# Attention and experts on one core: the product with V a pair later, three probability buffers, and another check of the weights' low halves

## The reference

```python
codes = jnp.sign(v) * FP4_GRID[idx]          # FP4_GRID = 0, 0.5, 1, 1.5, 2, 3, 4, 6
scale = jnp.exp2(e)                          # a power of two for each block of 32 rows
w = codes * jnp.repeat(scales, block_size, axis=0)
q = _mxfp4_matmul(x, wq_codes, wq_scales) + bq       # k, v alike
attn = jax.nn.softmax(einsum('bqhd,bkhd->bhqk', q, k) / sqrt(128), axis=-1)
out = einsum('bhqk,bkhd->bqhd', attn, v)
...
x = x + _layernorm(attention(_layernorm(x)))
x = x + _layernorm(experts(_layernorm(x)))
```

## Time and profile before

| | |
|---|---|
| Executions shown | 1331.55, 1329.47, 1333.42 us |
| Median | 1331.55 us |
| Span of the profiled execution (first to last instruction) | 1341.9 us |
| Own time of the profiled execution, beside its span | not given apart from the three above |
| PE busy | 1207.5 us (90%) |
| POOL, DVE, ACT busy | 931.0, 860.6, 825.8 us (69, 64, 62%) |
| First scores, scores of pair 12, last scores (pair 127) | 30.7, 142.3, 977.0 us |
| End of the last WO | 993.6 us |

### The profile page before, as it was taken

How to read it: one execution, slowest core, us unless ns; L and a number is a source line. 1 busy time by engine, 2 the same in 40 slices (tenths; PEclk the granted TensorE clock), 3 DMA queues, 4 the chain that set the end, 5 groups by cost and what they waited for, 6 DMA issues and landing times.

```text
span 1341.9 us, 25318 instructions
## 1 busy us (share of the span) xinstructions
PE 1207.5 (90%) x7852; PEld 844.1 (63%) x7852; DVE 860.6 (64%) x2297; ACT 825.8 (62%) x2128; POOL 931.0 (69%) x1130
## 2 busy tenths in 40 slices
PE   4889999999999999989999999998958799989995
PEld 1556666666666666657666666665635378777973
DVE  5898567687678768767876876777676233222226
ACT  3666678768777776877777677777745133223413
POOL 4896456678878877986888798688764624444557
PEclk9899999999999999999999999999989899999998
DMA  7774987755555354354534545434445359898676
GB/s 257 173 191 94 228 211 150 163 102 120 122 99 118 73 116 94 73 108 82 93 68 98 97 69 94 79 70 81 81 100 165 112 166 259 226 234 213 131 211 227
DMA packets 364678, 182.68 MB, mean 136 GB/s; under 512 B 287440, under 2 KB 343222, under 8 KB 364544
## 3 DMA queue, kind: packets, MB, share of 16 engines
q1 hardware_dynamic: 344960, 166.18, 52.5%
q0 software_dynamic: 16416, 11.70, 4.9%
q10 hardware_dynamic: 3168, 3.15, 0.7%
HBM read 75.32 MB, written 64.69 MB: 104 GB/s over the span
## 4 chain that ended last, share of the span: by engine, by line
PE 39%; DVE 18%; DMA 14%; POOL 13%; issue 7%; ACT 5%; another core or an unknown queue 2%; SPq 1%; ACTq 0%; POOLq 0%; DVEq 0%
DMA PT<-PH 8%; PE bank L1066 7%; PE bank L1037 6%; PE bank L1081 6%; DMA Y<-W,wix 5%; POOL PH L972 4%; POOL P L967 4%; PE bank L1052 4%; PE bank L1098 3%; PE bank L1206 3%; DVE nm L1455 3%; PE bank L1219 2%; POOL BUF L716 2%; PE bank L1130 2%
## 5 line engine op out<-in xcount | busy, mean ns | idle before, releaser
L967 POOL TENSOR_SCALAR P<-P,rr 128x256 f32<-128x256 f32 x512 | 249.2, 498 | 141.2 <-DVE rr L1451 132.2
L1308 ACT ACTIVATE P<-bank,nm 128x256 f32<-128x256 f32 x512 | 237.2, 468 | 149.2 <-DVE nm L1455 140.9
L972 POOL TENSOR_TENSOR PH<-P,PH 128x512 f16<-128x512 f32 x256 | 296.2, 1171 | 20.1 <-ACT PH L1317 19.1
L1037 PE MATMUL bank<-RB,W 128*128 128x512 f16 x1076 | 257.9, 382 | 7.2 <-ACT Sx L645 4.2
L716 POOL DMA_INDIRECT BUF<-RT,ix x192 | 197.8, 1030 | 91.3 <-issue 42.2
L1066 PE MATMUL bank<-RB 128*128 128x256 f32 x1024 | 245.7, 383 | 2.7 <-issue 2.5
L1081 PE MATMUL bank<-PT,RB 128*128 128x256 f16 x1536 | 197.2, 273 | 36.1 <-DMA PT<-PH 32.1
L1455 DVE TENSOR_REDUCE nm<-bank 128x2 f32<-128x512 f32 x256 | 174.3, 682 | 51.1 <-PE bank L1066 50.5
L1081 PEld LDWEIGHTS bank<-PT,RB 128*128 128x128 f16 x1536 | 145.1, 98 | 95.9 <-DMA PT<-PH 50.5
L1066 PEld LDWEIGHTS bank<-RB 128*128 128x128 f32 x1024 | 185.7, 191 | 26.2 <-issue 3.8
L1317 ACT ACTIVATE PH<-P 128x512 f16<-128x512 f32 x256 | 161.4, 630 | 55.7 <-POOL P L967 38.9
(11 more groups left out here) (207 smaller groups left out, 1600.0 us busy)
## 6 DMA issues: line engine op xcount, KB each, us to landing
RB<-in_ewT SPq DMA_DIRECT2D x24, 352.0 KB
BUF<-zrow SPq DMA_DIRECT2D x4, 1926.0 KB, 8.4
W<-BUF SPq DMA_DIRECT2D x64, 120.4 KB
HT<-in_ewT SPq DMA_DIRECT2D x18, 352.0 KB
HT<-in_wc SPq DMA_DIRECT2D x24, 256.0 KB, 4.3
HT<-in_ws SPq DMA_DIRECT2D x24, 256.0 KB, 4.7
Y<-zrow SPq DMA_DIRECT2D x10, 512.0 KB, 3.5
RB<-in_ewd SPq DMA_DIRECT2D x24, 176.0 KB
```

What stands on the lines that cost most here:

```text
L967: r = eng.tensor_scalar(p, p, rr[:, w % 4, t:t + 1], SP_, ALU.mult, ALU.mult)
L972: eng.tensor_tensor(PH[:, w % 2, 1, :], P[:, w % 2, :], PH[:, w % 2, 0, :], ALU.subtract).then_inc(s["pl"], 1)
L1037: r = eng.matmul(bk_[:, :], W[:, m, a, c * 2048 + h * 128:c * 2048 + (h + 1) * 128], XT[:, bp % 2, b, c, :], start=(k == 0), stop=(k == n ...
L1308: r = eng.activation(P[:, u % 2, t * 256:(t + 1) * 256], bS[u % 2][:, t * 256:(t + 1) * 256], ACT.Exp, bias=nm0[:, u % 4, t:t + 1], accum_ ...
```

## The change

`ORDER` moves PV two slots on (units w-3 and w-4 rather than w-1 and w-2), WO two slots (w-5, w-6), the halves of O likewise (ACT 3 to 5, DVE 4 to 6), and puts V between Q and K. `PH` and `PT` get a third buffer (`NPT`), which lies in `SSf`; the load that stood there is moved to SP's slot 232 and to `XN`. So the turning DMA of unit w waits for PV of w-3, and the high half of w for the DMA of w-3. `P` keeps two buffers, and Pool's order of work on probabilities is the same. The background tables are laid out anew; the 24 scatters, for one, stand in slots 34 to 59 rather than 32 to 55. The loop is two slots longer. The check of a job's low half is one `tensor_reduce` with max over its 256 words, to one column for each job; the sign bit is not cleared any more.

```diff
@@ -19,7 +19,7 @@
 E = 64
 CAP = 96
 NST = 8
-W_AT = (0, 0, 1, 2, 2, 3, 4, 5, 5, 6, 7, 7, 8, 9, 10, 10, 11, 12, 12, 13, 14, 15, 15, 16)
+W_AT = (0, 0, 1, 2, 2, 3, 5, 6, 6, 7, 7, 9, 10, 10, 11, 13, 14, 15, 15, 16, 17, 17, 17, 17)
 W_LEAD = (1, 1, 2)
...
-NOSIGN = 0x7FFF7FFF
...
+NPT = 3
...
-ORDER = {
-    "pe": ([("S", 0), ("S", -1), ("Q", -2), ("K", -2), ("WO", 4), ("WO", 3), ("V", -6), ("PV", 2), ("PV", 1),
-                ("bg", 0)],
-           [("bg", 0)]),
-    "act": ([("exp", 0), ("bg", 0), ("exp", -1)],
-           [("Q", -1), ("P", 1), ("V", -5), ("P", 0), ("O", 3), ("bg", 0)]),
-    "dve": ([("max", 0), ("O", 4), ("max", -1), ("bg", 0), ("recip", 0), ("bg", 0), ("bg", 0)],
-           [("bg", 0), ("recip", 0), ("K", -1), ("bg", 0), ("V", -5), ("bg", 0)]),
-    "pool": ([("bg", 0)],
-           [("norm", 1), ("norm", 0), ("P", 1), ("P", 0), ("bg", 0)]),
-    "sp": ([("bg", 0), ("T", 1)],
-           [("bg", 0), ("T", 1)]),
-}
+ORDER = {'pe': ([('S', 0), ('S', -1), ('Q', -2), ('V', -6), ('K', -2), ('PV', 4), ('PV', 3), ('WO', 6), ('WO', 5),
+         ('bg', 0)],
+        [('bg', 0)]),
+ 'act': ([('exp', 0), ('exp', -1), ('bg', 0)],
+         [('bg', 0), ('Q', -1), ('P', 1), ('V', -5), ('P', 0), ('bg', 0), ('O', 5)]),
+ 'dve': ([('max', 0), ('O', 6), ('max', -1), ('recip', 0), ('bg', 0)],
+         [('recip', 0), ('bg', 0), ('K', -1), ('bg', 0), ('V', -5), ('bg', 0)]),
+ 'pool': ([('bg', 0)], [('norm', 1), ('norm', 0), ('P', 1), ('P', 0), ('bg', 0)]),
+ 'sp': ([('bg', 0), ('T', 1)], [('bg', 0), ('T', 1)])}
...
-PE_AT = (17, 19, 23, 31)
-STORE_AT = (18, 20)
+PE_AT = (19, 20, 25, 33)
+STORE_AT = (24, 34)
...
-KEEP_AT = (22, 24)
+KEEP_AT = (19, 26)
...
-        "pool": ((11, 0), (11, 0), (11, 2), (11, 4), (32, 0), (33, 4), (34, 0), (37, 0), (37, 0), (38, 0),
+       'pool': ((13, 0), (13, 0), (13, 2), (13, 3), (34, 0), (35, 0), (36, 0), (39, 0), (39, 0), (39, 4),
+                (40, 0), (42, 0), (42, 0), (43, 1), (46, 0), (48, 0), (48, 0), (50, 0), (51, 4), (53, 0),
+                (53, 0), (53, 3), (53, 4), (54, 0), (56, 0), (56, 0), (58, 0), (59, 0))}}
...
+        SSh = SSf[:, :].bitcast(F16)
+        PHB = [PH[:, 0, :, :], PH[:, 1, :, :], SSh[:, 0:1024].rearrange("p (l n) -> p l n", l=2)]
+        PTB = [PT[:, 0, :, :, :, :], PT[:, 1, :, :, :, :],
+               SSh[:, 1024:2048].rearrange("p (l t c q) -> p l t c q", l=2, t=2, c=2)]
...
-        lowbits = C1[:, :, :].rearrange("p t e -> p (t e)").bitcast(U32)
+        lowmax = C1[:, 0, 0:32]
...
-        sdf = SSf[:, 0:768].rearrange("p (j n) -> p j n", j=3)
+        sdf = XN[:, 0:3, :]
...
                 eng.wait_ge(s["wl"], n + 1)
-                if n == 0:
-                    eng.tensor_scalar(lowbits, lo.bitcast(U32), NOSIGN, None, ALU.bitwise_and).then_inc(s["lf"], 1)
-                else:
-                    eng.wait_ge(s["lf"], n)
-                    eng.scalar_tensor_tensor(out=lowbits, in0=lo.bitcast(U32), scalar=NOSIGN, in1=lowbits,
-                                             op0=ALU.bitwise_and, op1=ALU.bitwise_or).then_inc(s["lf"], 1)
...
-                return eng.tensor_reduce(low1, lowbits, AX, ALU.max)
+                return eng.tensor_reduce(low1, lowmax, AX, ALU.max)
...
                 eng.wait_ge(s["pl"], w + 1)
-                if w >= 2:
-                    eng.wait_ge(s["pv"], w - 1)
-                eng.dma_start_transpose(PT[:, w % 2, :, :, :, :].rearrange("p l t c q -> p (l t c) q"),
-                                        PH[:, w % 2, :, :].rearrange("p l n -> p (l n)")).then_inc(s_pt[w % 2], 16)
+                if w >= NPT:
+                    eng.wait_ge(s["pv"], w - NPT + 1)
+                eng.dma_start_transpose(PTB[w % NPT].rearrange("p l t c q -> p (l t c) q"),
+                                        PHB[w % NPT].rearrange("p l n -> p (l n)")).then_inc(s_pt[w % NPT], 16)
...
+                if slot == 232:
+                    eng.wait_ge(s["xc"], XC.n)
                     eng.dma_start(sdf[:, 0:2, :], sdT[0:256, :].rearrange("(j p) n -> p j n", p=128)
...
-                eng.tensor_tensor(PH[:, w % 2, 1, :], P[:, w % 2, :], PH[:, w % 2, 0, :], ALU.subtract
+                eng.tensor_tensor(PHB[w % NPT][:, 1, :], P[:, w % 2, :], PHB[w % NPT][:, 0, :], ALU.subtract
...
-                eng.wait_ge(s_pt[u % 2], 16 * (u // 2 + 1))
+                eng.wait_ge(s_pt[u % NPT], 16 * (u // NPT + 1))
...
-                                       PT[:, u % 2, b, :, kc, :], start=(k == 0), stop=(k == 5))
+                                       PTB[u % NPT][:, b, :, kc, :], start=(k == 0), stop=(k == 5))
...
             def p_high(w):
+                if w >= NPT:
+                    eng.wait_ge(s_pt[w % NPT], 16 * (w // NPT))
                 eng.wait_ge(s["pn"], w + 1)
-                if w >= 2:
-                    eng.wait_ge(s_pt[w % 2], 16 * (w // 2))
-                eng.activation(PH[:, w % 2, 0, :], P[:, w % 2, :], ACT.Copy).then_inc(s["ph"], 1)
+                eng.activation(PHB[w % NPT][:, 0, :], P[:, w % 2, :], ACT.Copy).then_inc(s["ph"], 1)
```

More of the change, by code:

```diff
@@ L108 @@
 X_SHIFT = 12
-PE_AT = (17, 19, 23, 31)
-STORE_AT = (18, 20)
+PE_AT = (19, 20, 25, 33)
+STORE_AT = (24, 34)
 PROLOGUE = {"act": "wxwwxwxww", "dve": "xxxxxxxxxxxxxxxxxwxwxwwww"}
-KEEP_AT = (22, 24)
[L115 to L123, removed]
[6 rows of a table removed]
-        "act": ((9, 5), (9, 5), (9, 5), (10, 0), (15, 4), (16, 0), (16, 2), (17, 2), (18, 0), (19, 4), (24,
-                0)),
-        "pool": ((11, 0), (11, 0), (11, 2), (11, 4), (32, 0), (33, 4), (34, 0), (37, 0), (37, 0), (38, 0),
-                (38, 0), (40, 0), (41, 1), (41, 2), (43, 1), (45, 0), (46, 0), (46, 0), (46, 0), (49, 0), (49,
-                1), (49, 4), (49, 4), (51, 4), (52, 0), (54, 0), (54, 0), (55, 3)),
-    },
-}
+KEEP_AT = (19, 26)
+PLACE = {'x': {'dve': ((1, 3), (1, 5), (2, 1), (2, 3), (2, 4), (3, 0), (3, 2), (3, 3), (3, 3), (4, 4), (4, 4), (4, 4),
+               (4, 4), (5, 1), (5, 4), (6, 1), (6, 2), (12, 0), (14, 0)),
+       'act': ((6, 2), (7, 5), (8, 2), (10, 2), (11, 4), (13, 4)),
+       'pool': ()},
[7 rows of a table added]
+       'act': ((11, 3), (11, 5), (12, 0), (12, 0), (17, 5), (18, 0), (18, 2), (19, 1), (20, 0), (21, 6),
+               (26, 0)),
+       'pool': ((13, 0), (13, 0), (13, 2), (13, 3), (34, 0), (35, 0), (36, 0), (39, 0), (39, 0), (39, 4),
+                (40, 0), (42, 0), (42, 0), (43, 1), (46, 0), (48, 0), (48, 0), (50, 0), (51, 4), (53, 0),
+                (53, 0), (53, 3), (53, 4), (54, 0), (56, 0), (56, 0), (58, 0), (59, 0))}}
 def places(chain, base):
@@ L351, in build @@
         s_st = [sem(f"s_st{i}") for i in range(NST)]
-        s_pt = [sem(f"s_pt{i}") for i in range(2)]
+        s_pt = [sem(f"s_pt{i}") for i in range(NPT)]
         s_x1 = [sem(f"s_x1{i}") for i in range(2)]
@@ L541, in low @@
                 eng.wait_ge(s["wl"], n + 1)
-                if n == 0:
-                    eng.tensor_scalar(lowbits, lo.bitcast(U32), NOSIGN, None, ALU.bitwise_and).then_inc(s["lf"], 1)
-                else:
-                    eng.wait_ge(s["lf"], n)
-                    eng.scalar_tensor_tensor(out=lowbits, in0=lo.bitcast(U32), scalar=NOSIGN, in1=lowbits,
-                                             op0=ALU.bitwise_and, op1=ALU.bitwise_or).then_inc(s["lf"], 1)
+                eng.tensor_reduce(lowmax[:, n:n + 1], lo.bitcast(U32), AX, ALU.max).then_inc(s["lf"], 1)
             act_at, dve_at = (slot, slot) if n < NST else (slot + W_LEAD[1], slot + W_LEAD[2])
@@ L886, in _ @@
             eng.wait_ge(s["xc"], XC.n)
-            for k in range(2):
-                eng.wait_ge(s_pt[k], 16 * NI)
+            for k in range(NPT):
+                eng.wait_ge(s_pt[k], 16 * len(range(k, NU, NPT)))
             eng.wait_ge(s["pv"], NU)
```

## The result

The changed kernel took 1467.87 us in the median of four executions (1459.75 to 1469.95), the kernel before 1330.51 (1328.39 to 1333.42): a ratio of 1.1012, 95% interval 1.0976 to 1.1048. The forecast was 1466 us, range 1448 to 1491. The profiled execution is the shortest of the four: 1459.75 us, with a span of 1458.0 us and a clock of 0.992 (before 0.983). The other three had clocks of 0.985 to 0.988 and took 6.5 to 10 us more.

The account below looks back on a forecast made before the run. The prediction took PE's own work to bound the attention. From a span of 1341.9 us, -60 (waits) -7 (check and lag) +199 (passes) +2 (end) gave 1475.9, less 10.3 for span above median: 1466 us, range 1448 to 1491.

Parts of the forecast that it names:

- The sign bit: Check of low halves: -0.0 would set the number to 1 and send PE to the three-pass copy; chance 0.87.
- The price of the passes: Behind pair 12, three passes make a pair 8.23 us, not 6.50: 1.73 us for 115 pairs, +199 us.
- the 199 named as a sign: In the profile after, PE's busy time was to rise by some 199 us in total.
- The waits: PE behind pair 12: the lag and third buffer remove most of 66 us of waits, -60 us (bounds -66, -45).
- The early stretch: Pairs 0 to 12: cheaper check and lag together save 7 us (-2 if POOL alone holds it, -13 at most).
- The check itself: DVE's max over low halves, 22 jobs: near 407 ns each in place of 961, some 12 us of DVE.
- The jump: At the branch to the three-pass copy: the jump costs nothing that PE shows.
- The end: Last scores to last WO: two more slots and 0.44 us more a WO group, +2 us (bounds 0 and +5).
- The tail: Behind the end of the last WO: unchanged, 0 us.
- The first rival: Behind pair 12: the number stays 0, two passes, 18 of 66 us of waits kept, 1276 us (1256 to 1304); chance 0.11.

Follow-up runs that it names:

- abs_check: The changed kernel, with the check taking the maximum of absolute values of the 512 f16 numbers, so -0.0 counts as zero; 1328.41 us against 1348.63, ratio 0.9836.
- high_dve: The changed kernel with its raw check, but DVE writes the high halves by a multiplication in place of ACT's Copy; ratio 0.9874 to the kernel before.
- before_max: The kernel before with the changed kernel's check (raw words, sign included), old order and two buffers kept; 1481.89 us against 1348.63, ratio 1.0960.
- two_both: The changed kernel with its raw check, but both copies behind the branch make two passes; ratio 0.9803 to the kernel before.
- three_first: The changed kernel with the two copies behind the branch swapped, so three passes fall through and two are jumped to; one execution, 1461.08 us.
- before_abs: The kernel before with the check by absolute values, its order and two buffers kept; ratio 0.9980 to the kernel before.
- p_three: abs_check with a third buffer for P, the exponential's wait for POOL's low half one unit later; ratio 0.9845 to the kernel before.

## Why the prediction was right, and where it was not

**The sign bit** (0.87 for three passes): right, and shown: abs_check undoes it, high_dve finds its source. The Trainium skill's rule (ScalarE: Activation LUTs, "Free affine") was what no row of the kernel before could give; by what the two runs show, the result agrees with it. They show what Copy makes of -0.0, and not which step in ACT does it.

**The price of the passes**, +199 us: right. The pair is 8.24 us as the earlier trace rows had it. Pair 12 to the last scores took 964.7 us; 834.7 + 199.0 less all of the 66 us of waits is 967.7. PE's busy time rose by 173.8 us in all (1207.5 to 1381.3), and not by the 199 named as a sign: behind pair 12 it rose by 181, since each wait that goes takes the 0.16 us of overlap ahead of it out of the count, and in the early stretch it fell by 6.9.

**The waits**, -60 us: the size was near (834.7 + 199.0 - 964.7 = 69.0 gone, 9 more than said and 3 beyond the bound of 66; summed over the starts of PE's groups the waits of the kernel before are 69 too, so the block's own work had been put a little too high), the reason was wrong in the main. The step "That removes most of both waits, whatever else happens" credits the lag and the third buffer; the longer pair is named only as what makes the rest small. before_max shows that the longer pair does it alone: 1.73 us more against a mean wait of 27/35 = 0.8. Where the new order, with its third buffer and its tables, stands without the longer pair, at two passes (abs_check), the 26.8 us of PV's waits for `PT` are gone and 20.0 for the scores and V have come. The rows had it: a mean wait under half of the 1.73 us that each pair gained.

**The early stretch**, -7 us: measured -6.5, but by other parts than the prediction's, so the agreement is luck. (The lower clock of the earlier trace rows stood in the prediction only in the bound of -13.) Windows view of the stretch, before and with the change:

```profile
30.60:142.30 111.70, 101.27 (x571) 64.22 (x570) 93.60 (x160) 73.16 (x185) 90.64 (x95) 0.97 0.60 142
30.40:135.50 105.10, 94.35 (x546) 61.05 (x545) 80.76 (x160) 73.44 (x186) 87.77 (x95) 1.00 0.67 153
```

PE is busy for 6.9 us less, and idle for about as long (10.4 and 10.7 us). Of the 6.9 us, 2.6 are one pair's PV and WO, 24 matmuls, which the lag has moved to the end of the attention, where the time grows by it. The other 4 go with the clock, 0.97 before and 1.00 after: in the kernel before it was 0.50 from some 46.3 to 53.1 us, where the earlier trace rows stand, while in the changed kernel it didn't fall. two_both and three_first, which have the changed kernel's instructions in this stretch, ran it at 0.98 and 0.97; so these 4 us are put down to the one execution and not to the change. PE's idle time holds the jump's 3.1 us now, so the other waits fell by 2.7 us. The check's share of that is about 1.4 us by before_abs and before_max (8.9 and 9.1 us of idle time without the jump, beside 10.4, all three at a clock of 0.97), with one profile each.

The check itself is cheaper as predicted: L537 takes 420 ns in 22 jobs, where L546 took 961 and the estimate was 407; POOL's product is at 1265 ns, where it was 1453. Two rows of DVE's lines, 47 to 135 us:

```profile
L534 DVE SCALAR_TENSOR_TENSOR W<-HT,W 128x512 f16<-128x512 f32 x22 | 19.1, 869 | 0.4 <-ACT W L530 0.4
...
L537 DVE TENSOR_REDUCE C<-W 128x1 f32<-128x256 uint32 x22 | 9.2, 420 | 0.8
```

and one of POOL's, 47 to 84.9:

```profile
L526 POOL TENSOR_TENSOR HT<-HT 128x512 f32<-128x512 f32 x10 | 12.5, 1265 | 0.7 <-DMA HT<-in_ws 0.5 <-DMA HT<-in_os 0.2
```

The Trainium skill (VectorE: DVE Perf Modes, Rules for kernel authors) calls the reduction the slowest DVE op. The trace doesn't show that: over the same 256 words L546's shortest call took 424 ns and its longest 1380, while the reduction took 419 to 421 in all of its 32 calls.

**The jump**, "costs nothing that PE shows": wrong. It was read from a branch that fell through, and this one is taken: PE stands idle for 3.2 us there, which the -6.5 us of the early stretch already hold.

**The end**, +2 us: measured +5.2, just over the bound of 5; 2.6 of it are the pair's PV and WO that the early stretch lost. Timeline of PE from the last scores:

```profile
1100.21 1.89 PE L1058 MATMUL bank<-RB 128*128 128x256 f32 x8
...
1117.40 1.47 PE L1090 MATMUL bank<-W,O 128*128 128x256 f16 x12
1120.50 1.48 PE L1090 MATMUL bank<-W,O 128*128 128x256 f16 x12 [1.63 <-DVE O L1453]
1132.30 1.09 PE L1122 MATMUL bank<-HT,W 128*96 128x512 f16 x2 [10.32 <-DVE W L1476]
```

PE waits for DVE's step for O (L1453) four times there (0.67, 0.61, 0.69 and 1.63 us in this timeline), since with the deeper lag two more units' PV and WO come behind the last scores. The next operation stands 10.3 us off, as before.

**The tail**, 0: right for the change. But the 10.3 us by which the profiled span of before lay above its median were taken off the sum as if they held for the changed kernel too. By its own profile the change without the tail is -0.3 - 6.5 + 130.0 + 5.2 = +128.4 us, against +134 forecast; that the forecast of 1466 came within 2 us of the median is thus partly luck, with executions 10 us apart and tails 22. What isn't luck is the side and the size: three passes, at +199 us less the waits, are 130 of the 137 us.

**The first rival** (1276 us) was mis-sized: where it had "18 of 66" us of waits kept, abs_check keeps 49 of 69 by the starts of PE's groups (6.0 us in the block of pairs 64 to 80, where the kernel before has 9.8), and by ratio the time is 0.9836 x 1330.5 = 1309 us.

Of the kernels that can still make three passes where the weights need them, abs_check and p_three are the fastest, at 0.984 of the kernel before.

## What to carry to other kernels

A flag that a kernel computes from its data to choose a short path is part of its time: when the test of it is rewritten, ask first which inputs must still pass, signed zeros among them, and look in the timeline for which copy ran. Waits in a pipeline whose bound engine has little slack vanish when that engine's own period grows; don't credit them to whatever was changed in the same diff, but run the old order at the new period. A deeper lag moved the wait here to the next late steps, K's and V's on DVE. And where a short stretch comes out as forecast, split it into busy and idle time and read the clock of both executions before taking it as shown.
